# Inverse deviations of two layer normalisations: a power on GpSimd in place of a root on ScalarE and a reciprocal on VectorE

## The reference, cut to what matters

```python
def _layernorm(x, axis=-1, eps=1e-05):
    m = jnp.mean(x, axis=axis, keepdims=True)
    v = jnp.var(x, axis=axis, keepdims=True)
    return (x - m) / jnp.sqrt(v + eps)

x = _layernorm(x + gat_gat(x, ...), axis=-1)
x = _layernorm(x + max_block(x, ...), axis=-1)
```

## Time and profile before

| what | value |
|---|---|
| median of 3 runs | 6834.78 us (6834.69 to 6835.98) |
| the profiled execution, its own time | 6832.27 us |
| its span (first to last instruction) | 6830.1 us |
| mean granted TensorE clock | 0.618 of full speed |
| busy: PE, DVE | 5096.8 us (75%), 4105.4 us (60%) |
| busy: ACT, POOL | 4663.4 us (68%), 4931.9 us (72%) |

### The profile page before, as it was taken

The page is one execution under the profiler, slowest core; times in us unless marked ns, Lnnn a source line. Parts: engine busy times, 40 slices in busy tenths (PEclk is TensorE's granted clock), DMA queues, the critical chain, the costliest instruction groups (busy, mean ns, idle before and its releaser), DMA issues.

```text
span 6830.1 us, 136152 instructions
## 1 busy us (share of the span) xinstructions
PE 5096.8 (75%) x24591; PEld 4781.8 (70%) x24591; DVE 4105.4 (60%) x11895; ACT 4663.4 (68%) x10649; POOL 4931.9 (72%) x5211
## 2 busy tenths in 40 slices
PE   7988888888887798888888888764555556556557
PEld 6987888888887798887888788754455455455455
DVE  3655555555556565555555555665666666666667
ACT  5877777777776687777777777774555555555558
POOL 5777777777775777777777777557777777777772
PEclk6555555555555655555555555567888888878889
DMA  8544454445443654455445445365655665665564
GB/s 233 127 120 118 115 121 120 117 115 122 120 114 73 155 131 114 119 121 118 114 121 119 117 115 123 87 181 153 176 167 163 176 173 165 167 178 170 162 181 140
DMA packets 820306, 942.88 MB, mean 138 GB/s; under 512 B 185576, under 2 KB 549426, under 8 KB 819234
## 3 DMA queue, kind: packets, MB, share of 16 engines
q1 hardware_dynamic: 658962, 595.34, 31.2%
q0 software_dynamic: 159968, 334.75, 21.7%
q10 hardware_dynamic: 432, 2.45, 0.1%
HBM read 882.59 MB, written 49.44 MB: 136 GB/s over the span
## 4 chain that ended last, share of the span: by engine, by line
PE 22%; POOL 15%; issue 10%; DVE 9%; DMA 8%; DVEq 2%; ACT 1%; SPq 1%; POOLq 0%; ACTq 0%
POOL G L693 15%; PE bS L826 8%; PE bA L791 7%; DVE acc L1433 3%; DMA st<-d_neg 3%; DMA G<-table,idx 2%; DMA G<-ztable,idx 2%; PE bE L826 2%; PE bM L826 2%; DVE bA L1668 2%; DVE ch L1674 1%; PE bA L714 1%; PE bE L714 1%; DVEq L1433 1%; DVE G L1500 1%
## 5 line engine op out<-in xcount | busy, mean ns | idle before, releaser
L693 POOL DMA_INDIRECT G<-table,idx x3322 | 3135.6, 944 | 1049.8 <-issue 904.3
L826 PE MATMUL bS<-G,S 128*128 x8816 | 2040.0, 391 | 371.9 <-DVE acc L1433 221.5
L826 PEld LDWEIGHTS bS<-G,S 128*128 128x128 f32 x8816 | 1755.5, 280 | 492.5 <-issue 484.8
L693 POOL DMA_INDIRECT G<-ztable,idx x1661 | 1567.3, 944 | 524.0 <-issue 465.4
L1082 ACT ACTIVATE S<-iota_row,nd 128x128 f32<-128x128 f32 x5904 | 1864.5, 387 | 85.8 <-issue 41.1
L791 PEld LDWEIGHTS bA<-adst,st 128*128 128x128 f32 x7872 | 1797.1, 333 | 128.9 <-issue 125.6
L791 PE MATMUL bA<-adst,st 128*128 x7872 | 1698.9, 340 | 92.4 <-issue 70.1
L1433 DVE TENSOR_TENSOR acc<-acc,bS 128x136 f32 (+1 forms) x4408 | 1279.5, 290 | 574.9 <-DVE acc L1433 100.9
L1086 ACT ACTIVATE S<-S,one_col 128x512 f32<-128x512 f32 x1476 | 1065.3, 722 | 57.5 <-issue 8.9
L1068 ACT ACTIVATE st<-xr,neg_p 128x512 f32<-128x512 f32 x984 | 699.4, 711 | 524.4 <-DMA xr<-d_drel 337.8
L714 PE MATMUL bA<-ident,G 128*128 128x128 f32 x1664 | 332.1, 341 | 682.4 <-DVE ch L1674 563.7
(11 more groups left out here) (217 smaller groups left out, 3987.2 us busy)
## 6 DMA issues: line engine op xcount, KB each, us to landing
xr<-d_drel SPq DMA_DIRECT2D x984, 256.0 KB
xr<-in_ew SPq DMA_DIRECT2D x312, 256.0 KB
st<-d_neg SPq DMA_DIRECT2D x312, 256.0 KB
G<-table,idx POOLq DMA_INDIRECT x3322
isend<-in_ew SPq DMA_DIRECT2D x104, 256.0 KB
isend<-d_neg SPq DMA_DIRECT2D x104, 256.0 KB
G<-ztable,idx POOLq DMA_INDIRECT x1661
table<-G SPq DMA_DIRECT2D x48, 264.0 KB, 5.0
```

The source lines that it names most:

```text
L693: pool.indirect_dma_start(G[:, r, c, 0:width], None, from_table, bass.IndirectOffsetOnAxis(ap=idx[:, r, c:c + 1], axis=0)).then_inc(gather ...
L826: mm = pe.matmul(bank_of(l, u, r, k)[:, j * w:(j + 1) * w], S[:, onehots(r, i), s, :], Gf[:, bass.ds(chunk_at[0][s], w)], start=True, stop ...
```

## The change

It touches four places. The root on ACT is gone in both stages. DVE adds eps to the variance in place, behind a wait for its own `bn_aggr`, and only that addition raises `ln_in` or `f_std_in`. POOL raises the sum to the power -0.5 (`tensor_tensor` with a tile of -0.5, 128 x 4) and writes `rstd`; it takes over the wait that protects the two buffers of `rstd`. DVE's reciprocal and the wait between it and L1624 are gone. POOL's order: in the first stage the root of group g - 1 stands behind `own_rows(2, g)`; in `final` three `final_rows` come first, then root g and `final_rows(g + 3)` in turn. No DMA is added or removed. The tile `halves` (16 bytes a partition) replaces `eps` (4 bytes).

```diff
-        eps = sb("eps", [P, 1])
+        halves = sb("halves", [P, GT])
...
+            def roots(g, seen, made):
+                n = tiles_of(g)
+                pool.wait_ge(seen, g + 1)
+                if g >= 2:
+                    pool.wait_ge(*((o_made, NG + g - 1) if seen is ln_in else (f_y, g - 1)))
+                pool.tensor_tensor(rstd[:, g % 2, 0:n], mv[:, g % 2, 0:n, 1], halves[:, 0:n], ALU.pow).then_inc(made, 1)
...
             edge_gathers(1, table[1], TW)
+            for g in range(NG + 1):
+                if g < NG:
+                    own_rows(2, g)
+                if g >= 1:
+                    roots(g - 1, ln_in, ln_std)
+            edge_gathers(2, ztable, HID)
+            for g in range(3):
+                final_rows(g)
             for g in range(NG):
-                own_rows(2, g)
-            edge_gathers(2, ztable, HID)
-            for g in range(NG):
-                final_rows(g)
+                roots(g, f_std_in, f_std)
+                if g + 3 < NG:
+                    final_rows(g + 3)
...
-            def deviations(g):
-                n = tiles_of(g)
-                act.wait_ge(ln_in, g + 1)
-                act.activation(std[:, g % 2, 0:n], mv[:, g % 2, 0:n, 1], ACT.Sqrt, bias=eps[:, 0:1]).then_inc(ln_std, 1)
...
-                def deviation(g):
-                    n = tiles_of(g)
-                    act.wait_ge(f_std_in, g + 1)
-                    act.activation(std[:, g % 2, 0:n], mv[:, g % 2, 0:n, 1], ACT.Sqrt, bias=eps[:, 0:1]).then_inc(f_std, 1)
...
-            vec.memset(eps[:, :], EPS)
+            vec.memset(halves[:, :], -0.5)
...
                 for j in range(n):
                     ins = vec.bn_aggr(mv[:, g % 2, j, :], stats[:, g % 2, j, :])
-                ins.then_inc(ln_in, 1)
+                link(ins)
+                vec.tensor_scalar(mv[:, g % 2, 0:n, 1], mv[:, g % 2, 0:n, 1], EPS, None, ALU.add).then_inc(ln_in, 1)
...
-                link(vec.reciprocal(rstd[:, g % 2, 0:n], std[:, g % 2, 0:n]))
                 vec.scalar_tensor_tensor(nmr[:, g % 2, 0:n], mv[:, g % 2, 0:n, 0], -1.0, rstd[:, g % 2, 0:n],
                                          ALU.mult, ALU.mult).then_inc(ln_made, 1)
```

More of the change, by code:

```diff
@@ L206, in gnn_program @@
         mv = lnb[:, 256:256 + 4 * GT].rearrange("p (n t f) -> p n t f", n=2, t=GT)
-        std, rstd, nmr = (lnb[:, at:at + 2 * GT].rearrange("p (n t) -> p n t", n=2) for at in (384, 448, 512))
+        rstd, nmr = (lnb[:, at:at + 2 * GT].rearrange("p (n t) -> p n t", n=2) for at in (448, 512))
         has_t = lnb[:, 640:640 + P]
@@ L1183, in node_step @@
                         turned_rows(phase, g - 1)
-                    if g < NG:
-                        deviations(g)
             def node_tail(phase):
@@ L1258, in final @@
                 for g in range(NG + 5):
-                    if 4 <= g <= NG + 3:
-                        deviation(g - 4)
                     if g + 2 < SPARE:
@@ L1724, in rows @@
                         ins = vec.bn_aggr(mv[:, g % 2, j, :], stats[:, g % 2, j, :])
-                    ins.then_inc(f_std_in, 1)
+                    link(ins)
+                    vec.tensor_scalar(mv[:, g % 2, 0:n, 1], mv[:, g % 2, 0:n, 1], EPS, None, ALU.add).then_inc(f_std_in, 1)
                 def scales(g):
```

## The result

The changed kernel takes 6845.73 us (median of 20 runs, 6841.54 to 6849.83), the kernel before 6833.90 us in the same comparison: ratio 1.0018, 95% interval [1.0012, 1.0024]. It is slower by 12 us, where 6 us less were forecast. The profiled execution took 6844.98 us with a span of 6843.2 us, 13.1 us more than before.

The account below looks back on a forecast made before the run. No engine busy above 75%; DVE and ACT hold each other up in the first normalisation, DVE paces the final stage. -4 - 1.9 - 0.2 = -6 us from the profiled 6832.27 gives 6826, median 6829; range 6816 to 6858.

Parts of the forecast that it names:

- a difference from the stages outside, which nothing here touches: Sign of a wrong forecast: time changing outside the two normalisation stages, where the sum had no term.
- The end, -0.2 us: End of the final stage: ACT's last two groups start 0.2 us earlier without the root in front.
- The first stage, steps 1 to 18, -4 us: First normalisation: four groups take 24.6 us against 25.5, -0.9 us, over 4.5 such stretches.
- L1624's wait: First normalisation, DVE: L1624 meets POOL's L657 and waits an estimated 0.4 to 0.5 us.
- the border's 2.5 us: First normalisation, part borders: DVE's five logits meet POOL's root, L652 and L657, some 2.5 us against 0.92 before.
- The root, 0.43 us: The power on POOL, priced like a 128 x 32 copy at 0.43 us; beyond 1 us would be wrong.
- the bound of POOL's block: First normalisation: beyond a root of about 0.9 us POOL becomes the bound, some 25 us for each further us.
- The last six groups, -1.9 us: End of the first normalisation: 26.9 us against 28.8, POOL's pace 4.4 us a group, ACT's 3.4.
- The final rounds, 0: Final stage: addition replaces reciprocal, root hidden in POOL's idle time; zero, between -0.5 and +1 us over 25 rounds.
- Rival 1: First normalisation: a slow root on POOL makes the kernel slower, some 6880 us with 3 us; chance 0.24.
- Rival 2: First normalisation: collisions of DVE with POOL do not come, 6811 us; chance 0.16, including cases between below 6821.
- Rival 3: First normalisation: PE partly keeps ACT's saving from DVE, 6835 us; counted within no measurable change, chance 0.60.

Follow-up runs that it names:

- one_pow_b: The kernel before plus a single 128x4 power as POOL's last instruction, on its own tile, nothing waiting for it: 6888.44 us against 6838.98, ratio 1.0074.
- one_product: The kernel before plus a single 128x4 product as POOL's last instruction, on its own tile: 6830.01 us against 6830.40, ratio 1.000.
- pow_before_l2_b: The changed kernel plus one more 128x4 power on POOL ahead of layer 2's gathers: 6833.26 us, against 6844.71 for after_third.
- after_third: The changed kernel run again with nothing altered: 6844.71 us, ratio 1.0018 to the kernel before.
- C: Experiment on the end: the kernel before plus a one-number write by POOL behind the last scales: 6843.57 us against 6838.98, ratio 1.0007.
- mult_root: The changed kernel with a product in place of the power in both normalisations, on a slower chip: ratio 1.0009 to the kernel before.
- root_twice: The changed kernel with the first normalisation's power computed twice, once into an unread tile: 6864.12 us, ratio 1.0043 to the kernel before.

## Why the prediction was wrong

The forecast was 6 us less, and the kernel is slower by 12 us. That the time lies in the range is luck: its upper part was kept for a slow root in the first stage, and what filled it came from two other places. By its steps:

- **"a difference from the stages outside, which nothing here touches"**: this is the step that failed: the sum put the stages outside at zero, without a reason beyond that their instructions are the same, and my own list named a difference there as what would make the forecast wrong. Layer 2 costs 11.3 us more through 8 ns on each gather; one_pow_b against one_product and pow_before_l2_b against after_third show the power as cause, though not by what mechanism. None of the three rivals had it.
- **The end, -0.2 us**: it became +5.4, the second step that failed. I saw POOL idle at the end and priced its new work by what waited for it. Among the engines only DVE waits for the last root, and ACT behind it; but the end of the execution stands 9.2 us behind it (C). ACT's earlier start could not show beside that.
- **The first stage, steps 1 to 18, -4 us**: from the first to the last part's first L652 it is 119.97 us (4463.89 to 4583.86) against 125.31 (4448.98 to 4574.29): -5.3 us. The pace was forecast as 24.6 us for four groups and is 24.04. Of its terms, L1624's wait of 0.7 us (0.85 less its own 0.16) is above my 0.4 to 0.5, though at borders it has none, and the border's 2.5 us are one hit of 1.1 (L1575, 1.34 against 0.23 for its kin): the logits pass beside the power. The table loads are gone: ACT's busy time fell by 22.0 us (4663.4 to 4641.4), loads and roots together.
- **The root, 0.43 us**: it is 1.03 us, beyond my own mark of "wrong beyond 1 us". That its length did no harm is not my model's merit: by it, 1.03 us should have brought the sum to about +1 us (4 for 0.5 to 0.9 us, 3 beyond). The model held the root for an instruction that blocks DVE and put the bound of POOL's block at 0.9 us. The block behind the root is 3.8 us in place of 4.3, the period 5.27, so by the rows the bound lies near 1.5 us, an estimate; mult_root shows that shorter is not better. Beyond it I had 25 us a us plus the last groups; root_twice gives 18.7 us for 1.0 us.
- **The last six groups, -1.9 us**: from the last weights to the last L1176, 25.82 us (4583.86 to 4609.68) against 28.84: -3.0. POOL's pace is 4.36 us (roots at 4587.22, 4591.58, 4595.93), forecast 4.4; ACT's loop 3.4 to 3.6, forecast 3.4. The store behind it takes 0.7 us longer. By all this the gathers start 7.6 us earlier in the stage's own count (-5.3 - 3.0 + 0.7).
- **The final rounds, 0**: 4.83 us against 4.80, +0.03, so within the bound of +1 over 25 rounds. The root is hidden in the round as said; what it brings is the end above.
- **Rival 1**, a first call of about 6 us (the Trainium skill, "GPSIMD Engine Reference", Instruction dispatch): the first root starts at 4471.22, takes 1.05 us, and L652 follows at 4472.26. No such pause is there. The power does have a cost that its own row doesn't show, but a different one. **Rival 2** was half right: the logits' collisions at the border stay away, and one hit of 1.1 us is left there. **Rival 3** did not come: DVE kept the saving.

So the two stages' own work came out at -7.6 + 0.3 us, near the -6 of the sum. The rest is +11.3 and +5.4, where the sum had no term, and the 3.6 us of the first two columns, which I take for scatter; together the 13.1 us of the spans.

## What to carry to other kernels

When an engine gets a kind of operation that its program did not have, price also what that program does elsewhere: multiply a few ns by the count of its most frequent instruction. Here one further power ahead of layer 2's gathers gave the 11.5 us back, and in the kernel before a power ahead of all gathers cost nothing that could be measured. Compare gathers or other frequent groups by median per stage before looking at the stage that was changed, and look at which engine's program ends last: work given to GpSimd near the end moves the 9 us behind it too, however idle it was, and costs time once they end behind everything else.

## What was unexpected of the hardware

- A power in GpSimd's program: in layer 2 and the maximum layer, indirect DMAs of GpSimd issued before it is first executed take 952 or 956 ns in place of 944, and none behind it does. In layer 1 this was so in one kernel of six. With all 4983 of them slow it cost 49 us.
- A power of 128 x 4 takes 1.03 us on GpSimd, one of 128 x 2 0.70, a product of 128 x 4 0.2; while a power runs, VectorE's two-operand instructions take their usual 0.23 us, beside GpSimd's adds up to 1.3.
- A drain of GpSimd ends 9.0 us behind GpSimd's last instruction (20 traces), and no execution ended before it; where GpSimd is done early enough, the span ends 1.5 us behind the last store.
